# Residual sum and depth convolutions of a convolution network as one stage per image on the chip

## What is computed

```python
def _L1_conv_ref(x, A, conv_w, conv_b, gamma, beta):        # graph convolution
    y = relu(conv(x, conv_w) + conv_b)
    y = einsum('bctn,nm->bctm', y, A)
    ...                                                      # y normalised over the batch
    return relu(y * gamma + beta)

def offset_branch(x, dw_w, dw_b, bn_g, bn_b, pw_w, pw_b):   # in _L2_conv_ref
    h = conv2d(x, dw_w, dw_b, padding=1, groups=x.shape[1])  # depth convolution 3 x 3
    h = relu(batchnorm(h, bn_g, bn_b))
    return conv2d(h, pw_w, pw_b, padding=0)
```

## Time and profile before

| | us |
|---|---|
| three executions | 4402.07, 4393.8, 4390.53 |
| median | 4393.8 |
| profiled execution | 4387.39 |
| its span | 4385.3 |
| PE / DVE / ACT / POOL busy | 3644.4 / 2559.5 / 2639.7 / 2443.9 |
| `residual_norm`, from the first load to the last of its work | about 226 |
| `depth_conv`, with its start and end | about 560 |

### The profile page before, as it was taken

The page is one execution under the profiler, slowest core; times in us unless marked ns, Lnnn a source line. Parts: engine busy times, 40 slices in busy tenths (PEclk is TensorE's granted clock), DMA queues, the critical chain, the costliest instruction groups (busy, mean ns, idle before and its releaser), DMA issues. The chain is left out here.

```text
span 4385.3 us, 142489 instructions
## 1 busy us (share of the span) xinstructions
PE 3644.4 (83%) x59682; PEld 2156.9 (49%) x59682; DVE 2559.5 (58%) x5104; ACT 2639.7 (60%) x2951; POOL 2443.9 (56%) x1787
## 2 busy tenths in 40 slices
PE   6866548723799996569999999999999999999588
PEld 5755444423233332246655556555565555655222
DVE  5401646633233335757777777777777777776555
ACT  5600103323122225469999989999899999998442
POOL 0010220001000004769999999999999999999500
PEclk9955658955899998879999999999999999999799
DMA  3264649999877776532221221212212122020585
GB/s 99 58 136 117 193 113 238 222 322 279 198 219 216 216 212 260 190 83 59 57 69 45 68 59 35 69 45 68 59 35 69 45 66 59 17 71 22 137 211 125
DMA packets 675526, 532.88 MB, mean 122 GB/s; under 512 B 39434, under 2 KB 600714, under 8 KB 667050
## 3 DMA queue, kind: packets, MB, share of 16 engines
q1 hardware_dynamic: 556444, 386.26, 34.1%
q10 hardware_dynamic: 108560, 105.02, 7.8%
q0 software_dynamic: 9984, 33.56, 2.3%
HBM read 338.51 MB, written 186.19 MB: 120 GB/s over the span
## 5 line engine op out<-in xcount | busy, mean ns | idle before, releaser
L1563 POOL TENSOR_SCALAR df_t<-df_t 128x1536 f32<-128x1536 f32 x1536 | 2200.0, 1570 | 51.3 <-ACT df_t L1573 51.2
L1744 PE MATMUL df_o<-df_t,df_zs 128*32 128x128 f32 x36864 | 1326.8, 277 | 42.6 <-POOL df_t L1563 27.9
L1616 DVE TENSOR_SCALAR df_t<-df_d 128x512 int32<-128x512 int32 x1536 | 1062.6, 692 | 487.8 <-PE df_d L1700 483.6
L1573 ACT ACTIVATE df_t<-df_a 128x1024 f32<-128x1024 f32 x1024 | 1051.7, 1027 | 204.4 <-PE df_a L1700 201.9
L1744 PEld LDWEIGHTS df_o<-df_t,df_zs 128*32 128x32 f32 x36864 | 914.1, 109 | 470.7 <-issue 263.8
L1700 PE MATMUL df_d<-df_ix,net_sel 11*128 11x512 bf16 x1536 | 592.7, 386 | 2.5 <-DVE df_t L1616 0.9
L1573 ACT ACTIVATE df_t<-df_z 128x1024 f32<-128x1024 f32 x512 | 525.8, 1027 | 36.3 <-PE df_z L1700 5.4
L1577 ACT ACTIVATE df_zs<-df_z 128x864 f32<-128x864 f32 x512 | 452.9, 884 | 2.0 <-PE df_z L1724 2.0
L1700 PE MATMUL df_a<-df_ix,net_sel 11*128 11x512 bf16 x2048 | 398.3, 386 | 46.7 <-DMA df_ix<-offset 46.6
L1724 PE MATMUL df_z<-net_Z,df_x 32*128 32x288 f32 x4096 | 393.2, 429 | 18.0 <-ACT df_x L1591 9.6
L1089 POOL CAST of_parts<-of_t_o 128x512 bf16<-128x512 f32 x64 | 64.0, 1000 | 615.6 <-ACT of_t_o L1066 586.8
(11 more groups left out here) (228 smaller groups left out, 4749.2 us busy)
## 6 DMA issues: line engine op xcount, KB each, us to landing
gc_x<-x SPq DMA_DIRECT2D x240, 128.0 KB, 4.8
dc_x<-x SPq DMA_DIRECT2D x240, 128.0 KB, 3.3
dc_xt<-x_2t SPq DMA_DIRECT2D x240, 128.0 KB, 4.7
fw_x<-in_x SPq DMA_DIRECT2D x32, 512.0 KB, 6.7
iv_x<-in_x SPq DMA_DIRECT2D x64, 256.0 KB, 4.7
x<-iv_x POOLq DMA_DIRECT2D x64, 256.0 KB, 5.0
y<-gc_o ACTq DMA_DIRECT2D x64, 256.0 KB, 5.5
r_y<-y SPq DMA_DIRECT2D x8, 2048.0 KB, 13.8
```

Source lines behind the costliest of these rows:

```text
L1563: g.tensor_scalar(t, t, 1.0, 0.0, ALU.min, ALU.max).then_inc(hat_p, 1)
L1573: act.activation(T[:, n % 2, 3 * i:3 * i + 2], src, ACT.Abs).then_inc(a_read, 1)
L1616: v.tensor_scalar(T[:, n % 2, 3 * i + 2].bitcast(I32), ps_d[:].bitcast(I32), 0x7fffffff, None, ALU.bitwise_and).then_inc(d_read, 1)
L1744: mm = pe.matmul(ps_o[32 * q:32 * q + 32, 0:P], Zs[:, n % 2, q, 32 * k:32 * k + 32], T[:, n % 2, 3 * i + x, P * q:P * q + P], start=(k == ...
```

## The change

`residual_norm` and `depth_conv` become one stage, `sum_and_depth`. Its pieces:

- x2 of an image stays on chip after the sum. DVE writes it normalised into XA (`normalise`), ACT copies XA shifted into XB (`move`, two copies of 64x4096). The turned copy still goes through DRAM: PE transposes, ACT copies, POOL writes, SP reads it back once into TA, DVE normalises it in place (`normalise_turned`) and ACT makes TB (`move_turned`).
- Work of image b+1 stands between the convolutions of image b: the sum, statistics, mean and variance in kind 0, `normalise` and `move` at the end of kind 0, the transposes in kind 1, `move_turned` at the end of kind 2.
- A kind is done for all 8 chunks of an image before the next kind. PSUM has 5 banks for results, 2 for transposes.
- A chunk of a kind is 3 taps x 3 matmuls: one with 64 array columns from XA (or TA) and two with 32 from XB (or TB).
- Stores go in pieces of 128x1024 on SP's queue, from four tiles. The results are in the residue order 1, 2, 3, 0; `offsets` stores its result with the residues turned by one, and `load_plain` in `deformable` loads in two DMAs in place of one. LX, LY and LP are twice as wide, made by twice as many small operations.
- The loop over the images is written out.

```diff
-def residual_norm(nc, sems, name, y, coef, x, x_out, pair, GS, turn=None):
+def sum_and_depth(nc, sems, y, coef, x, x_out, xt, pair, GS, wt, hx, hy, up, stx, sty):
...
+                def keep_sum(b):
+                    sp.wait_ge(added, b + 1)
+                    for q in range(4):
+                        sp.dma_start(x_out[b][q], X[32 * q:32 * q + 32, b % 2].rearrange("c (j w) -> c j w", w=W)).then_inc(x_sent[b % 2], 16)
...
+                def load_turned(b):
+                    sp.wait_ge(t_sent, 64 * (b + 1))
...
+                def move_turned(b):
+                    if b:
+                        a.wait_ge(conv, number(b, 0, 0))
+                    a.wait_ge(t_normed, b + 1)
+                    for r, j in ((slice(0, 64), 0), (slice(64, 128), 1)):
+                        a.activation(TB[r, j:j + J, 1:W + 1], TA[r, b % 2, :, 1:W + 1], ACT.Copy).then_inc(t_moved, 1)
...
+                def turn(b, m):
+                    n = NC * b + m
+                    if m == 0:
+                        pe.wait_ge(added, b + 1)
+                    if n >= 2:
+                        pe.wait_ge(t_done, n - 1)
...
+                def convolve(b, k, c):
+                    n = number(b, k, c)
+                    bank = ps[n % 5]
...
+                    if n >= 5:
+                        pe.wait_ge(o_done, n - 4)
+                    w_ = wt[kinds[k][0]]
+                    for d in range(3):
+                        for r, t, i in ((slice(0, 64), ta, j), (slice(64, 96), tb, j + 1), (slice(96, 128), tb, j)):
+                            mm = pe.matmul(bank[r, :], w_[:, d, r], t[:, i:i + 4, d:d + W], start=(d == 0), stop=(d == 2))
+                    mm.then_inc(conv, 1)
...
+                for b in range(B):
+                    more = b + 1 < B
+                    for c in range(NC):
+                        convolve(b, 0, c)
+                        if more and c == 3:
+                            means(b + 1)
+                        if more and c == 5:
+                            variances(b + 1)
+                    for c in range(NC):
+                        convolve(b, 1, c)
+                        if more:
+                            turn(b + 1, c)
+                    for c in range(NC):
+                        convolve(b, 2, c)
...
-                        sp.dma_start(off[b][:, :, q, :], parts[32 * q:32 * q + 2 * K9, b % 2]).then_inc(sent[b % 2], 16)
+                        sp.dma_start(off[b][:, :, (q + 1) % 4, :], parts[32 * q:32 * q + 2 * K9, b % 2]).then_inc(sent[b % 2], 16)
...
-                sp.dma_start(UT[:].rearrange("p j w -> p (j w)")[:, r], up[b][:, r]).then_inc(ut_in[2 * c // NCH], 16)
+                    for here, there in ((slice(32, 128), slice(0, 96)), (slice(0, 32), slice(96, 128))):
+                        sp.dma_start(UT[here].rearrange("p j w -> p (j w)")[:, r], up[b][there, r]).then_inc(ut_in[2 * c // NCH], 16)
```

More of the change, by code:

```diff
@@ L787, in _ @@
+                for k in range(2):
+                    sp.wait_ge(x_sent[k], 64 * (B // 2))
+                for k in range(4):
+                    sp.wait_ge(o_sent[k], 16 * (NC * NK * B // 8))
             @block.gpsimd
             def _(g):
[L789 to L800, removed]
+                for t in (XA, XB, TA, TB):
+                    g.memset(t[:], 0.0).then_inc(set_, 1)
@@ L812, in finish @@
[L812 to L841, removed]
+                def rectify(b):
+                    a.wait_ge(y_in, 32 * (b + 1))
+                    a.activation(Y[:], Y[:], ACT.Relu, bias=coef[:, 1:2], scale=coef[:, 0:1]).then_inc(relu, 1)
@@ L843, in _ @@
             @block.vector
             def _(v):
[L845 to L871, removed]
@@ new lines, in _ @@
+                add(0)
+                stats(0)
+                mean(0)
+                variance(0)
+                normalise(0)
+                normalise_turned(0)
+                for b in range(B):
+                    more = b + 1 < B
+                    if more:
+                        add(b + 1)
+                    for c in (0, 1):
+                        count(b, 0, c)
+                    if more:
+                        stats(b + 1)
+                    for c in (2, 3):
+                        count(b, 0, c)
+                    if more:
+                        mean(b + 1)
+                    for c in (4, 5):
+                        count(b, 0, c)
+                    if more:
+                        variance(b + 1)
+                    for c in (6, 7):
+                        count(b, 0, c)
+                    if more:
+                        normalise(b + 1)
+                    for c in range(NC):
+                        count(b, 2, c)
+                    if more:
+                        normalise_turned(b + 1)
@@ L873, in _ @@
             @block.tensor
             def _(pe):
-                pe.wait_ge(c_in, 16)
[L876 to L888, removed]
-                        pe.wait_ge(steps, ST * n + 2 + 10)
-                        alone(pe, passed)
-                        pe.matmul(ps[:, 0:1], pr[:], ag[:, 0:1], start=True, stop=True).then_inc(sums, 1)
-                        pe.wait_ge(steps, ST * n + 2 + 14)
-                        alone(pe, passed)
-                        pe.matmul(ps[:, 1:2], pr[:], dev[:], start=True, stop=True).then_inc(sums, 1)
```

364 lines of the change are left out of this document (212 added, 152 removed).

## The result

The changed kernel takes 4868.2 us (median; 4867.4 to 4873.5), the kernel before 4392.2 beside it: ratio 1.108, 95% interval 1.106 to 1.111. It is slower, by 476 us. 4880 was forecast.

The account below looks back on a forecast made before the run. PE was taken to fill the new stage: 929.5 + 3 + 1163.5 + 34 + 8 = 2138 for the last convolution, +481, with +3 and +5 +489, so 4876, median 4880 us. Own range 4825 to 4910; for 8 in 10, 4315 to 4910.

Parts of the forecast that it names:

- The price of a tap: Convolutions on PE: 0.86 for 64 columns, 0.86 for two of 32, two width changes of 0.15, 2.02 us together.
- The 0.10 of the range's lower end: Convolutions on PE: a width change at 0.10 us, the last pass's own drain counted apart, giving 1106 us and 4825.
- Transposes between the convolutions: PE, new stage: 56 groups of four transposes, each 0.43 plus one more width change, 0.6, together 34 us.
- Waits hidden: New stage: PE needs 150 us per image, ACT 41 and DVE 26, so their work and both new waits hide.
- rival 2: New stage: array emptied at width changes and low clock for good, a tap 3.72, about 5880 us; chance 0.10.
- The start: New stage, before the convolutions: nothing hides this work, PE starts its first convolution near 929.5, at the low clock costing 3.
- The stages in front: Before the new stage: six more small matmuls and 12 operations in `load_weights`, +5 us.
- The end: After the last matmul: last result, store and landing, 4.8 us today; store twice as large and on SP, +3.
- Offsets: Turned order of `offsets` and second DMA in `load_plain`: nothing, as `deformable` has its DMA engines busy 19%.
- The sum: Whole kernel: last convolution at 2138 instead of 1656.8, +481, with +3 and +5 +489: 4876, median 4880 us.
- Rival 1: Convolutions on PE: different widths stand side by side, PE then waits for its feeders; 4354, or 4360 median; chance 0.30.
- Rival 3: Convolutions on PE: widths side by side but each change still costs 0.15, 668 us of chunks, about 4465; chance 0.05.

Follow-up runs that it names:

- e2: Changed kernel with each chunk's nine matmuls reordered, three of 64 columns first, then six of 32: 4769.2 us, ratio 1.086.
- e3: Changed kernel with every convolution matmul cut in two of 256 columns of data, order 64, 32, 32 kept: 5017.8 us, one execution.
- e7: Changed kernel with the relu of image 1 moved behind ScalarE's copies of image 0 into XB: 4870.3 us, one execution.
- e10: Kernel of e9 with the next image's x2 store moved to mid kind 1 and image 1's loads held for image 0's turned copy: 4239.6 us, ratio 0.964.
- e1: Changed kernel with each tap's 64-column matmul written as two of 32, so all four have one width: 4370.7 us, ratio 0.996.
- e4: Kernel before with the second 64-column matmul of each depth convolution tap written as two of 32: 5037.8 us, one execution.
- e5: Changed kernel with all widths 32 and the next image's work moved so that PE should not wait for it: 4267.9 us, ratio 0.972.
- e9: Kernel of e5 with y and x loads issued by GpSimd instead of SyncE, ahead of the turned copy's store: 4278.4 us, ratio 0.975.

## Why the prediction was right

- **The price of a tap.** 2.02 forecast, 1.98 measured. The step that carried the forecast was to read 0.15 from changes whose columns overlap and to take it for columns apart. The changed kernel, e2 and e3 all bear it out. The size was a little too large, 0.13 on the mean: 192 x 0.10 = 19 us too many. One of its two sources was weaker than it looked: in the earlier trace rows the matmuls behind the change also have 11 rows of the array and another number format, so that row does not price a change of width alone. The 0.10 of the range's lower end stands in no row; the measured price lies above it.
- **Transposes between the convolutions.** 0.6 forecast; 1503.51 to 1504.09 is 0.58, and it includes the change that the convolution would have had.
- **Waits hidden.** Forecast for PE's waits within the images: none. Measured: 4.8, once. The granted clock was 0.99, so rival 2 did not happen.
- **The start.** 929.5 forecast, 949.6 measured, which is 67 after the stage's first load where 55 to 56 were forecast. Of the 20 between the two, 8.7 is the stages in front: the first load of the stage was issued at 882.6 in place of 873.9. The other 11.4 is the relu of image 1: its y was forecast for 918 and came at 938.5, 12 late beside those 8.7. The first 4 of these come before the store of x2: the sum of image 0 ended at 912.0 (899.5 and 8.7 were forecast), for it waited until 907.6 for x, where the forecast took x to be in as soon as today. The rest is the rate: my sum priced the store and y by their bytes at the 289 GB/s of the earlier trace rows, and from 912 to 938.5 the DMAs moved 216 GB/s; which of the transfers beside them takes the difference was not tried. e7 shows that in this order of work an earlier first convolution was worth nothing.
- **The stages in front.** +5 for `load_weights`; `graph_conv` loads its first x 11.7 later in this trace (662.3 before, 674.0), but 5.5 to 15.0 later in the others with this stage (667.9 in e3, 677.3 in e10). Part of that comes back in `graph_conv`. The term was too small, and scatters.
- **The end.** +3 forecast; from the last matmul's end (2139.5) to the next stage's first work are 3.9, where it was 4.8: -1.
- **Offsets.** Forecast 0. In this trace `offsets` is 7.5 longer (214.0 from first load to `deformable`'s first work, 206.5 before). But e1, with the turned order, has 207.1, and e4, which has the old one, 210.6. So most of this is the scatter of executions; a microsecond or two for the turned order is not excluded. From there to the end the trace is 2.8 shorter.
- **The sum.** From the first convolution to the last were 1189.9 in place of 1208.5, -18.6; -4 for the end, +11.4 and +3.7 for start and stages in front, +7.5 - 2.8 behind: the errors add to -3, and the span grew by 486.4 where 489 was forecast. That the total fits to 3 us is luck of signs: single terms are off by up to 19. Its last step is off by itself: 4876 and 6.4 are 4883, not 4880. The measured median is 12 below the 4880, most of it because the forecast put the median 6.4 above the profiled execution, as in the kernel before, and it lies 5.3 below it. The mechanism was right and not only the total: widths one after the other, 0.13 a change, no waits, the upper clock.
- **Rival 1** was wrong only in its condition. With that met (e1), 4370.7 was measured where it gave 4360, and its 114 us of waits were 122; the first convolution came at 945.8, 16 later than it had, which is more than the 11 between the two times.
- **Rival 3** (side by side, with changes) is ruled out by the starts in the changed profile, 1.00 and 0.98 apart, and by e2: 5.42 a chunk, the two streams one after the other.

## To carry to other kernels

Before an even tiling is replaced by one with fewer but unequal matmuls, count the changes of width in PE's order: each cost 0.12 to 0.15 us here, and what has different widths runs in a row where equal widths ran side by side. Splitting the wide matmul into narrow ones of the common width costs nothing on PE (0.43 for four passes of 32 columns as for two of 64). And where many transfers want to go at once, try first to move what nobody waits for behind the stores that free the result tiles: another queue alone brought nothing here (e5 to e9), the move and the later loads of image 1 brought 39 us on top of it (e10), and the move without the other queue was not run.

## What the runs showed beyond that

- Weight loads of another width are not pulled ahead of running matmuls: they start with their own matmuls (1501.52 and 1502.52 in the changed kernel), where within one width a load starts 0.43 ahead.
- The time that a DMA takes to issue is not fixed by the DMA: the same four stores of x2 held SyncE's queue for 7.5 in e5, 27.2 in e9 (7.8 there for the last image, without loads beside it) and 7.4 in e10, by what else was under way. Whether the queue stands for its own entries or for the engines' was not tried.
- PE was granted 0.99 of the full clock through 1190 us in which its width changed about once per us. After a real wait it was not. In e1, after 12.0 us of idle time, passes of 0.60 take 1.07 for the next 6 us; the granted clock is 0.50 from 1154 to 1160 (1.2 GHz) and 1.00 behind it:

```profile
1153.61 0.59 PE L1013 MATMUL rd_s<-rd_ag,rd_pr 128*128 128x1 f32 x2 [12.01 <-DVE rd_ag L936]
1154.13 1.07 PE L1045 MATMUL rd_c<-rd_xa,net_LX 128*32 128x512 f32 x2
...
1160.10 0.61 PE L1045 MATMUL rd_c<-rd_xa,net_LX 128*32 128x512 f32 x2
```
